# A transformer block on one core: other orders at both ends of the program, and the row pass of the first normalisation on ScalarE

## What is computed

```python
mod = (silu(c) @ wmod)                      # sa, ca, ga, sb, cb, gb: six rows of 256 per batch
ga, gb = sign-preserving max(|.|, 0.25)
h = layernorm(x) * (1 + ca) + sa
x = x + ga * attention(h)                   # 16 heads of 16, causal, with a slope per head and distance
h = layernorm(x) * (1 + cb) + sb
x = x + gb * ffn(h)                         # 704 wide; silu(gate) * up, then down
```

## Time and profile before

| | us |
|---|---|
| median of 3 runs | 3705.48 (3704.08 to 3707.86) |
| the profiled execution, its own time | 3703.08 |
| its span, first to last instruction | 3700.9 |

### The profile page before, as it was taken

The page is one execution under the profiler, slowest core; times in us unless marked ns, Lnnn a source line. Parts: engine busy times, 40 slices in busy tenths (PEclk is TensorE's granted clock), DMA queues, the critical chain, the costliest instruction groups (busy, mean ns, idle before and its releaser), DMA issues.

```text
span 3700.9 us, 56917 instructions
## 1 busy us (share of the span) xinstructions
PE 3520.1 (95%) x20920; PEld 1879.2 (51%) x20920; DVE 3027.4 (82%) x5935; ACT 1912.3 (52%) x3503; POOL 1286.7 (35%) x918
## 2 busy tenths in 40 slices
PE   4999999999999999999999999999999999999977
PEld 2335554555555455454544555454555544555445
DVE  9887878788887888878788887888878788887846
ACT  3465555545555555555555555555555555555531
POOL 5123324243332524324242332424324243341223
PEclk7899999999999999999999999999999999999988
DMA  7243423313233332323323233332333323332010
GB/s 129 44 77 49 64 53 62 63 32 71 47 68 55 61 59 44 66 49 61 63 36 66 48 68 55 61 59 44 66 51 60 63 42 60 55 58 47 22 28 12
DMA packets 158184, 205.32 MB, mean 55 GB/s; under 512 B 44164, under 2 KB 98004, under 8 KB 157908
## 3 DMA queue, kind: packets, MB, share of 16 engines
q1 hardware_dynamic: 157908, 201.69, 31.4%
HBM read 63.65 MB, written 17.89 MB: 22 GB/s over the span
## 4 chain that ended last, share of the span: by engine, by line
PE 84%; DVE 10%; ACT 3%; issue 2%; POOL 1%; DMA 0%; SPq 0%; ACTq 0%; POOLq 0%; DVEq 0%
PE banks L706 14%; PE banks L688 13%; PE banks L730 13%; PE banks L825 8%; PE banks L832 8%; PE banks L848 7%; PE banks L757 5%; PE banks L806 3%; PE banks L788 3%; DVE banks L1135 2%; PE banks L841 2%; PE banks L691 2%; ACT arena L905 2%; DVE tm L1108 1%; PE banks L735 1%
## 5 line engine op out<-in xcount | busy, mean ns | idle before, releaser
L905 ACT ACTIVATE arena<-banks 128x512 f32<-128x512 f32 (+1 forms) x2432 | 1265.1, 583 | 869.5 <-PE banks L691 438.0
L1135 DVE CUSTOM_DVE_ANT_0 banks<-banks,mask 128x640 f32<-128x640 f32 (+3 forms) x1024 | 1032.8, 1043 | 211.1 <-PE banks L730 205.2
L730 PE MATMUL banks<-ka,qa 102*128 102x512 bf16 (+3 forms) x3072 | 761.0, 332 | 55.0 <-DVE top L1135 40.2
L688 PE MATMUL banks<-qa,ka 105*128 105x512 bf16 (+3 forms) x3072 | 791.1, 330 | 17.5 <-ACT arena L905 7.0
L706 PE MATMUL banks<-arena,va 128*17 128x512 f32 (+3 forms) x6144 | 645.9, 494 | 5.5 <-ACT arena L905 4.5
L688 PEld LDWEIGHTS banks<-qa,ka 105*128 105x128 bf16 x3072 | 270.4, 98 | 480.8 <-ACT arena L905 194.2
L730 PEld LDWEIGHTS banks<-ka,qa 102*128 102x128 bf16 x3072 | 258.7, 99 | 430.9 <-DVE top L1135 92.9
L1133 DVE TENSOR_REDUCE top<-banks 128x2 f32<-128x768 f32 (+3 forms) x384 | 389.9, 1043 | 87.6 <-PE banks L735 78.9
L1040 POOL TENSOR_TENSOR hid<-hid,tm 128x704 f32<-128x704 f32 x128 | 214.9, 1679 | 707.2 <-DVE hid L1109 707.2
L848 PE MATMUL banks<-wdT,hqT 128*128 128x256 f32 x1536 | 369.0, 391 | 5.2 <-ACT hqT L948 4.5
L825 PE MATMUL banks<-wguT,xqT 128*128 128x352 f32 x1024 | 336.1, 466 | 0.9 <-ACT xqT L939 0.9
(11 more groups left out here) (150 smaller groups left out, 4541.1 us busy)
## 6 DMA issues: line engine op xcount, KB each, us to landing
qa<-parts SPq DMA_DIRECT2D x384, 128.0 KB, 4.5
ka<-parts SPq DMA_DIRECT2D x384, 128.0 KB, 5.2
xa<-in_x SPq DMA_DIRECT2D x16, 1024.0 KB, 5.3
onT<-oT SPq DMA_DIRECT2D x256, 64.0 KB, 4.0
rsumT<-rsum_dram SPq DMA_DIRECT2D x64, 256.0 KB
xr<-in_x SPq DMA_DIRECT2D x64, 256.0 KB, 2.7
out_x<-xr SPq DMA_DIRECT2D x64, 256.0 KB, 4.7
ffn_rows<-rows_dram SPq DMA_DIRECT2D x16, 384.0 KB, 5.1
```

The costliest lines, as they stand in the source:

```text
L688: mm = pe.matmul(ps[:, m * w:(m + 1) * w], ka[g][0:KT, h, kt * P:(kt + 1) * P], qa[g][0:KT, h, q0:q0 + w], start=heads < G and m == 0, sto ...
L730: mm = pe.matmul(ps[:, at:at + z - a], qa[g][0:KS, h0 + m, qt * P:(qt + 1) * P], ka[g][0:KS, h0 + m, a:z], start=qt > 0 and m % paired == ...
L905: nc.scalar.activation(probs[:, s % P_SLOTS, j * heads:(j + 1) * heads, 0:w], ps[:, 0:heads * w].rearrange("p (h q) -> p h q", h=heads), A ...
L1135: nc.vector.tensor_tensor_reduce(out=ps, in0=ps, in1=mask[:, S - w:S], scale=1.0, scalar=MASKED, op0=ALU.add, op1=ALU.max, accum_out=tops) ...
```

## The change

Four things are done, and the due times of many jobs (`SHIFT`) are set anew with them.
1. N3 moves from VectorE's `normal_rows` to ScalarE: `Identity` with scale `rs` and bias `ms`, where `ms` = -mean * rs is one more small step of VectorE at the end of N2.
2. In the planner WQ jobs come after POOL's second split (no wait is written for it in the program).
3. For the last group of the last batch (`HALVED`) the normalisation is done by column halves, each after its own copy: DEN, NUM, RD, RDW, RBC, MUL twice on half the columns, output pairs 0 and 1 after the first, 2 and 3 after the second, and LR in two halves.
4. The rows for the second normalisation get two buffers and are loaded when batch b-2's last rounding is over, the gate row gb alone (FGATE) after batch b-1's last DN. The buffer `obg` goes: OB writes into `ga_row`, after WG, and GROW waits for the last FOLD.

```diff
+HALVED = (B - 1, NG - 1)
-    PATIENCE = {"ACT": 0.8, "POOL": 0.05, "SP": 0.3}
+    PATIENCE = {"ACT": 0.8, "POOL": 0.05, "SP": 0.5}
...
             p.add("DVE", ("N2", b), 2.2, at + 0.06 * L, ("DVE", ("N1", b, 1)))
             for h in range(2):
-                p.add("DVE", ("N3", b, h), 1.75, at + 0.07 * L + h, ("DVE", ("N2", b)), ("DVE", ("N3", b, 0)) if h else None)
+                p.add("ACT", ("N3", b, h), 2.4, at + 0.07 * L + h, ("DVE", ("N2", b)), ("ACT", ("N3", b, 0)) if h else None)
...
+                    if (b, g) == HALVED:
+                        normalise(b, g, due, c)
+            if (b, g) != HALVED:
+                normalise(b, g, due)
...
-            p.add("DVE", ("WQ", 0, n), 5.1, 60.0 + 16.0 * n, ("DVE", ("WQ", 0, n - 1)), ring=None)
+            p.add("DVE", ("WQ", 0, n), 5.1, 60.0 + 16.0 * n, ("DVE", ("WQ", 0, n - 1)), ("POOL", ("SPL", 0, 1)), ring=None)
...
-        p.add("SP", ("FROW", b), 0.7, at + L, ("POOL", ("RES", b - 1, T - 1)), lag=3.0)
+        p.add("SP", ("FROW", b), 0.7, at + 0.5 * L, ("DVE", ("XQ", b - 2, NPAIR - 1)), lag=7.0)
+        p.add("SP", ("FGATE", b), 0.7, at + L, ("DVE", ("DN", b - 1, T - 1)), lag=4.0)
...
-            pe(("O", b, r), 1.75, at + 2.0 + r, ("POOL", ("MUL", b, 0)), ("POOL", ("MUL", b, 1)), ("POOL", ("WG", b)),
+            half = (r // 2,) if b == HALVED[0] else ()
+            pe(("O", b, r), 1.75, at + 2.0 + r, ("POOL", ("MUL", b, 0)), ("POOL", ("MUL", b, 1, *half)), ("POOL", ("WG", b)),
...
-        p.add("DVE", ("LR", b), 2.4, at + 6.0, *(("DVE", ("O", b, r)) for r in range(NPAIR)))
+        for half in (0, 1) if b == HALVED[0] else ((),):
+            mine = range(NPAIR) if half == () else (2 * half, 2 * half + 1)
+            p.add("DVE", ("LR", b) if half == () else ("LR", b, half), 2.4, at + 6.0, *(("DVE", ("O", b, r)) for r in mine))
...
+                        elif r == 2 and b == HALVED[0]:
+                            pe.wait_ge(normal, b * C + C + 1)
...
+                    if kind == "N3":
+                        act.wait_ge(row_scales, b + 1)
+                        for t in range(4 * e[2], 4 * e[2] + 4):
+                            ins = nc.scalar.activation(xa[:, t, :], xa[:, t, :], ACT.Identity, bias=ms[:, t:t + 1],
+                                                       scale=rs[0][:, t:t + 1])
+                        ins.then_inc(xn_ready, 1)
+                        continue
...
+                if k == 0:
+                    nc.vector.scalar_tensor_tensor(out=ms[:, :], in0=mv[k][:, :, 0], scalar=-1.0, in1=y,
+                                                   op0=ALU.mult, op1=ALU.mult).then_inc(row_scales, 1)
...
-                    elif kind == "N3":
-                        normal_rows(range(4 * e[2], 4 * e[2] + 4))
```

More of the change, by code:

```diff
@@ new lines, in attention, with normalise @@
+            if (b, g) != HALVED:
+                normalise(b, g, due)
+    def normalise(b, g, due, *half):
+        old = (b, g, half[0] - 1) if half and half[0] else (b, g - 1) if g else (b - 1, NG - 1)
+        done = [("ACT", ("CO", b, g, c)) for c in (half or range(2))]
+        p.add("SP", ("DEN", b, g, *half), 0.7, due, *done, ("DVE", ("RD", *old)), lag=4.0)
+        p.add("SP", ("NUM", b, g, *half), 2.6, due + 1, *done, ("PE", ("O", b - 1, NPAIR - 1)), ("PE", ("WT", 0, GU // 2)), lag=7.0)
+        p.add("DVE", ("RD", b, g, *half), 0.4, due, ("SP", ("DEN", b, g, *half)), ("SP", ("RDW", *old)))
+        p.add("SP", ("RDW", b, g, *half), 0.7, due, ("DVE", ("RD", b, g, *half)), ("SP", ("RBC", *old)), lag=6.0)
+        p.add("SP", ("RBC", b, g, *half), 0.7, due, ("SP", ("RDW", b, g, *half)), ("POOL", ("MUL", b, g // 2 - 1) if g >= 2 else ("MUL", b - 1, C - 1)), lag=7.0)
@@ L305, in normalise @@
         if g % 2:
-            p.add("POOL", ("MUL", b, g // 2), 2.4, due + 10.0, *((("SP", (k, b, n)) for n in (g - 1, g) for k in ("NUM", "RBC"))), lag=8.0)
+            p.add("POOL", ("MUL", b, g // 2, *half), 2.4, due + 10.0, *(("SP", (k, b, g - 1)) for k in ("NUM", "RBC")),
+                  *(("SP", (k, b, g, *half)) for k in ("NUM", "RBC")), lag=8.0)
     def weights():
         for n in range(GU // 2 + 1):
-            p.add("DVE", ("WQ", 0, n), 5.1, 60.0 + 16.0 * n, ("DVE", ("WQ", 0, n - 1)), ring=None)
+            p.add("DVE", ("WQ", 0, n), 5.1, 60.0 + 16.0 * n, ("DVE", ("WQ", 0, n - 1)), ("POOL", ("SPL", 0, 1)), ring=None)
@@ L371, in feed_forward @@
                 pe(("DN", b, t), 2.75, late + 14, ("ACT", ("HT", b, t, 1)), ("PE", ("DN", *tile(t - 1))), ring="D", on="DVE",
-                   takes_cost=0.47, then=(("POOL", ("RES", *tile(t - 2))),))
+                   takes_cost=0.47, then=(("POOL", ("RES", *tile(t - 2))), ("SP", ("FGATE", b))))
                 p.add("POOL", ("RES", b, t), 0.8, late + 16, ("DVE", ("DN", b, t)), ("POOL", ("RES", *tile(t - 1))))
@@ L424, in adaln_block @@
         ga_row = sb("ga_row", [P, D])
-        ffn_rows = sb("ffn_rows", [P, 3, D])
-        cb_row, sb_row, gb_row = (ffn_rows[:, n, :] for n in range(3))
-        obg = sb("obg", [P, D])
+        ffn_rows = [sb(f"ffn_rows{n}", [P, 2, D]) for n in range(2)]
+        gb_row = sb("gb_row", [P, D])
         xb = [sb(f"xb{n}", [P, 2 * D]) for n in range(2)]
@@ L593, in _ @@
                             sp.wait_ge(rsums_ready, n)
-                        sp.dma_start(sums[:, :], oT[HD:P:P // G, :]).then_inc(sums_in, 16)
+                        sp.dma_start(sums[:, 0:G * S // P if c is None else G * BANK // P], oT[HD:P:P // G, queries]).then_inc(sums_in, 16)
                     else:
@@ L618, in _ @@
                         sp.wait_ge(normal, b * C)
-                    sp.dma_start(rsumT[half:half + 64, :], rsum_dram[g].unsqueeze(1).broadcast_to((G, HD, S))).then_inc(rsumT_in, 16)
+                    width = S if c is None else BANK
+                    sp.dma_start(rsumT[half:half + 64, queries],
+                                 rsum_dram[g][:, queries].unsqueeze(1).broadcast_to((G, HD, width))).then_inc(rsumT_in, 16)
             for r in range(NPAIR):
@@ L1158, in run @@
                             dve.wait_ge(rsums_out, 16 * n)
-                        nc.vector.reciprocal(rsums[:, :], sums[:, :]).then_inc(rsums_ready, 1)
+                        nc.vector.reciprocal(rsums[:, 0:w], sums[:, 0:w]).then_inc(rsums_ready, 1)
                     elif kind == "N1":
@@ L1205, in run @@
                         if r == 0:
-                            dve.wait_ge(ffn_rows_in, b * 16 + 16)
+                            dve.wait_ge(ffn_rows_in[b % 2], b // 2 * 16 + 16)
+                        cb_row, sb_row = (ffn_rows[b % 2][:, n, :] for n in range(2))
                         if b or r >= 2:
```

112 lines of the change are left out of this document (65 added, 47 removed), and 3 rows, old and new, of the table SHIFT.

## The result

The changed kernel takes 3688.1 us (median of 6 runs, 3686.0 to 3691.6) beside 3707.4 for the kernel before (6 runs on the same chip): a ratio of 0.995, 95% interval 0.9937 to 0.9963, so 19 us less (14 to 23). Forecast was 33 less.

What follows compares the result with a forecast made beforehand. TensorE was taken to bound the kernel, busy 95% of the span, with time to win mainly at both ends. 3703.1 - 12 (start) - 21 (end) + 0 (middle) = 3670, 3672 us on the median's scale; range 3643 to 3700.

Steps and rivals of the forecast that it cites:

- What bounds the kernel: TensorE works 3337 of 3420 us in the middle; idle time to win lies mostly before 140 us and after 3560 us.
- Order of the start: Batch 0: WQ 0 and 1 until 74.9 us, scores at 75, WQ 2 to 5 scattered behind; score start 20 us earlier.
- 12 of the 20 us stay: Start: of 20 us earlier scores 12 are kept, as four owed WQ take 20.6 us of VectorE; bounds 0 and 22.
- rival 3: Start's gain given back: owed WQ stop group 1's copies, late move into onT near 140 to 170 us; 3684, chance 0.14.
- The middle at 0: 140 to 3560 us: row pass on ScalarE mostly hidden, other edits add nothing worth counting; 0 us, range -30 to +20.
- The sum: 3703.1 - 12 - 21 + 0 = 3670, on the median's scale 3672 us; this forecast's chance 0.48.
- The row pass's own duration: ScalarE, first normalisation: 0.58 us per activation, 2.3 us per half, 4.7 per batch; ends 3.1 and 6.3 per batch.
- Rival 2: Middle gains as well: VectorE, 3 us lighter per batch, releases score matmuls in time; 25 us off, 3647, chance 0.20.
- The end at 21: Last group in halves: gate matmul 20 us earlier, 1 extra cost, 2 from the clock; 21 us, bounds 8 and 28.
- the lower bound of 8: End gains only 8 us if VectorE is busy with batch 14's hidden blocks until 3561, making half 0 late.
- the chances of faster: Rivals 1, 2, 3 and half of 4 count as faster: 0.86, with same 0.06 and slower 0.08.

Runs made afterwards that it cites:

- x1: Changed kernel with the quantisation of raw weight tiles 2 to 5 left out, orders and waits kept (work incomplete): 3681.8 us, ratio 0.9936.
- e1: Changed kernel with the last three raw weight tiles in the first hqT buffer, so NUM needn't wait for them; new planner orders: 3688.9 us, ratio 0.9959.
- e6: Changed kernel with the last three raw weight tiles in the first hqT buffer and NUM's wait removed, planner's orders kept: 3691.7 us, ratio 0.9956.
- b2: Kernel before with only the dependency that puts weight quantisations behind the first key splits, new order: 3707.9 us, ratio 1.0013.
- e4: Changed kernel without the dependency that puts weight quantisations behind the first key splits: 3706.4 us, ratio 1.0001.
- e2: Changed kernel with the row pass back on VectorE, right behind the scales, other orders kept: 3731.7 us, ratio 1.0085.
- e3: Changed kernel with the last group of batch 15 normalised in one piece: 3709.5 us, ratio 1.0009.
- b1: Kernel before with only the row pass of batches 1 to 15 moved to ScalarE, in one piece, other orders kept: 3720.8 us, ratio 1.0045.
- b4: Kernel before with the weight quantisation dependency and the last three raw weight tiles in the first hqT buffer, new orders: 3710.9 us, ratio 1.001.
- e8: Changed kernel with the planner's due times and patience of the kernel before: 3758.4 us, ratio 1.0141.

## Why the prediction was right and where it was off

Its sign and its range held; the forecast of 3672 was 16 us too low. Point by point:

- **What bounds the kernel.** Borne out: idle time fell only at the two ends, 28 us of it.
- **Order of the start.** Scores at 75 and exponents near 105 were read right to a us, and so were WQ 0 beside the splits and the value projection in idle time.
- **12 of the 20 us stay.** This term was the most mis-sized, and its mechanism was wrong. Of 20.4 us at the first copy 3.2 are left at the end of batch 0 and 1.5 at that of batch 1. The owed quantisations took 5 us (x1). The wait behind onT, on which rival 3 rests, took nothing: the late move that it named is there, at 209.8, and two experiments that remove the wait (e1, e6) gain nothing. In idle time 10.2 us did stay, near the 12. What the prediction had no term for is busy time: the same 2462 matmuls were busy 8.7 us longer, with 59.0 us at the lower level for 47.1. By the weighted sum above (1.91 us where the clock was low, 1.05 where it wasn't) those 11.9 us more would cost some 5 us, an estimate from these numbers. b2 and e4 have the same sign (20.3 and 13.6 us more at the lower level, 12.2 and 7.7 more busy). The prediction had read 0.59 and 0.66 for the clock of the start, and still took a us of idle time won there for a us of time won. No run changes the clock alone, so this stays a reading of the traces.
- **The dependency's worth.** Taking it out costs 18 us (e4), alone it gives nothing (b2). Both hold, since each time the planner makes another order for batches 0 and 1: e4's is 12.4 us behind the kernel before at the end of batch 1, b2's 6.7, and only the whole change is 1.5 ahead.
- **The middle at 0.** From 500 to 3400 us as taken: 66.3 us idle for 65.2. From the last copy of batch 1 to that of batch 14 it lost 2.7 us, within the spread. But the attention of batch 15 takes 195.4 us for 192.2. That is so in e1 to e4, e6 and x1 to 0.1 us, and not in the kernels from before (b1, b2, b4: 192.2); e8, with the old due times, has 193.3. So most of these 3 us go with the new due times, which the prediction had passed over as moving instructions past one another.
- **The sum** came near rival 3 (3684), but by another cause. That the range took it in is owed to its width, not to the mechanism.
- **The row pass's own duration.** 2.08 us for a block of four, 0.52 each (forecast 0.58, bounds 0.38 and 0.79), 4.1 per batch. By the figures of the Trainium skill, "ScalarE: Activation LUTs", section "What ACT_TABLE_LOAD costs", the estimate for an ACTIVATE of this form is 585 ns alone and 492 in a row, so 2.06 us for four. The trace agrees with 2.08. That the pass is hidden held too, but as a property of its place: 0.88 us per batch where it stands in one piece (b1), 0 where it stands in two.
- **Rival 2 (25 us more in the middle).** Fell: VectorE is 33 us lighter from 500 to 3400, and TensorE's waits for it are the same. Which tile waits is indeed set by order.
- **The end at 21.** Nearly right: 18.0 us behind the last copy, and by the experiment that undoes the halves 15.4 in the trace and 21 between the medians. The gate matmul was to come 20 us earlier; behind the last copy it came 19.9 earlier. The clock's part was taken too small: 2 us, at most 5. The 356 matmuls behind the last copy are busy 6.8 us less, at 27.1 us on the lower level for 40.2; the mean granted clock there rose from 0.80 to 0.86. Two details were wrong: half 0's projection was to start at 3557 and started at 3562.6, behind the last weighted sum in TensorE's order, and its sum had to wait for batch 14's hidden blocks on VectorE, the condition that the lower bound of 8 had named.
- **Small slips.** TensorE's work of batch 14 ended at 3570.2 (the projection at 3573.97 less its 3.73 of waiting), not at 3568. And the chances of faster add up to 0.87.

What stays open: why the matmuls up to batch 1 are busy longer by some 3 us more than that estimate, which of the new due times cost what, and what the kernel would take with neither dependency nor halves. b1 shows 9.0 us lost by batch 1 for the row pass alone, but in one piece and another order. Nor is it known whether an order exists with the early start and the gaps of the kernel before; no kernel tried beats the changed one with its work complete.

## What to carry to other kernels

A long piece of side work costs by its place, not by its length: the same row pass cost TensorE 2.6 us a batch, 0.9 or nothing, depending on what stood behind it, so split it and look at what is queued behind it before moving it to another engine. When an order is made by a planner from all costs and due times, read the new order through every stretch and not only at the place that was edited, because an effect there can be larger than the edit's own. And judge a gain between points at which the same work is done, by idle and by busy time: one copy alone can be late by mere reordering, and idle time alone hid that the same matmuls took 8.7 us longer at one end and 6.8 less at the other.

## What the runs showed of the hardware

VectorE's instructions stretch beside GpSimd's splits. GpSimd in e4:

```profile
167.99 2.27 POOL L1051 TENSOR_TENSOR xa<-xa,parts 128x1024 f32<-128x1024 f32 x1
...
172.00 2.63 POOL L1057 TENSOR_TENSOR parts<-xa,parts 128x1024 bf16<-128x1024 f32 x1
```

and beside each of them VectorE's tensor-tensor instruction of 128x704, 2.69 us (rows above), which takes 0.89 us with GpSimd idle (at 209.45 in the changed kernel). Two instructions of the feed-forward's normalisation took 3.57 us beside a split for 0.87 without (e8, and the changed kernel at 3571.4). The Trainium skill, "GPSIMD Engine Reference", section 8, states contention with VectorE instructions that have two inputs in SBUF; the trace agrees, and the factor is 3 to 4 for these. GpSimd's own instruction of that form takes 2.13 us at 201.2 in the changed kernel, so it lost little (7 and 23%).

The clock fell in the midst of a busy stretch: in the changed kernel TensorE paused 0.46 to 0.90 us before each of its groups from 206.6 to 211.7, and the mean granted clock from 200 to 220 us is 0.69 between stretches of 0.99 and 0.96; the clock record has the lower level from 207.8 to 221.4. In the kernel before, that stretch has 0.90.

And the same matmuls are busy for longer or shorter by what clock they are granted: behind the last copy 356 matmuls took 102.2 us with 40.2 at the lower level in the kernel before, and 95.4 with 27.1 in the changed one.
